# Searched network of a gated cross-attention stack: both halves of the probability transposes run back to back, each half in a score memory pair of its own

## The reference, cut to what matters

```python
for c in range(NUM_NOD):                     # 6 nodes
    q = ew[c, 0] * (nodes[in_q] @ We[eq] + be[eq])
    k = ew[c, 1] * (nodes[in_k] @ We[ek] + be[ek])
    v = ew[c, 2] * (nodes[in_v] @ We[ev] + be[ev])
    o = _mha(q, k, v, Wq[c], Wk[c], Wv[c], Wo[c])   # softmax(qh kh / sqrt(32)) vh, 8 heads, then @ wo
    nodes[c] = act_w[c] * o + q
...
return _layernorm(nodes[5], ln_g, ln_b)
```

## Time and profile before

| | |
|---|---|
| time, median of 3 runs | 3070.01 us |
| span of the profiled execution, first to last instruction | 3069.1 us |
| TensorE matmuls (PE) | 2945.7 us busy, 96% of the span |
| TensorE weight loads (PEld) | 2275.7 us, 74% |
| VectorE (DVE) | 2030.9 us, 66% |
| ScalarE (ACT) | 1448.5 us, 47% |
| GpSimd (POOL) | 650.4 us, 21% |
| searched network | about 816 to 1954 us of the span |

### The profile page before, as it was taken

How to read it: one execution, slowest core, us unless ns; L and a number is a source line. 1 busy time by engine, 2 the same in 40 slices (tenths; PEclk the granted TensorE clock), 3 DMA queues, 4 the chain that set the end, 5 groups by cost and what they waited for, 6 DMA issues and landing times. The chain is left out here.

```text
span 3069.1 us, 61161 instructions
## 1 busy us (share of the span) xinstructions
PE 2945.7 (96%) x23332; PEld 2275.7 (74%) x23332; DVE 2030.9 (66%) x4378; ACT 1448.5 (47%) x2845; POOL 650.4 (21%) x952
## 2 busy tenths in 40 slices
PE   8997999989899999999999999799999999899999
PEld 6874656567799999999999999577777777556444
DVE  5773111138577887788888877566767666589664
ACT  3431111126455555555555555476666666556000
POOL 4565000046100220013012200212212112036000
PEclk9997999999899999999999999899999999899999
DMA  9643233249300000000000000000000000337100
GB/s 292 214 128 106 82 117 110 88 144 299 104 1 2 1 2 1 2 1 1 2 1 2 1 2 1 24 25 22 17 22 22 17 22 17 106 108 227 51 14 21
DMA packets 79537, 185.47 MB, mean 60 GB/s; under 512 B 12981, under 2 KB 23202, under 8 KB 78916
## 3 DMA queue, kind: packets, MB, share of 16 engines
q1 hardware_dynamic: 62708, 141.50, 14.3%
q10 hardware_dynamic: 10208, 25.30, 2.8%
q0 software_dynamic: 6336, 14.76, 1.7%
HBM read 150.26 MB, written 27.79 MB: 58 GB/s over the span
## 5 line engine op out<-in xcount | busy, mean ns | idle before, releaser
L2792 DVE CUSTOM_DVE_ANT_0 probs<-ps,add 112x375 f32<-112x375 f32 x512 | 258.9, 544 | 82.7 <-PE ps L2945 76.0
L2871 ACT ACTIVATE probs<-probs,neg_top 112x375 f32<-112x375 f32 x512 | 278.5, 600 | 63.5 <-DVE neg_top L2792 60.1
L1734 DVE TENSOR_TENSOR hidden<-gated,ps 128x512 f32<-128x512 f32 x64 | 44.0, 687 | 294.7 <-PE ps L1777 294.7
L2972 PEld LDWEIGHTS ps<-ident,probs 112*125 112x125 f32 x1536 | 196.8, 188 | 44.4 <-issue 16.7
L2351 DVE TENSOR_REDUCE top<-ps 112x16 f32<-112x1792 f32 x96 | 194.2, 2023 | 46.1 <-PE ps L2590 45.9
L2972 PE MATMUL ps<-ident,probs 112*125 112x112 f32 x1536 | 219.7, 279 | 1.8 <-DVE probs_t L2799 1.8
L3416 PE MATMUL ps<-we,xn_t 128*128 128x512 f32 x448 | 201.9, 614 | 1.7 <-PEq L846 0.9
L2367 DVE TENSOR_TENSOR probs<-probs,inv_sum 112x1792 f32<-112x1792 f32 x96 | 196.0, 2042 | 3.3
L2355 DVE TENSOR_TENSOR probs<-ps,top 112x1792 f32<-112x1792 f32 x96 | 194.3, 2024 | 3.3
L2363 DVE TENSOR_REDUCE row_sum<-probs 112x16 f32<-112x1792 f32 x96 | 193.9, 2020 | 3.2 <-ACT probs L2475 3.2
L2558 PE MATMUL ps<-ident,probs 112*112 112x112 f32 x1536 | 179.8, 260 | 8.2 <-ACT probs_t L2470 7.3
(11 more groups left out here) (464 smaller groups left out, 6276.8 us busy)
## 6 DMA issues: line engine op xcount, KB each, us to landing
ctx_t<-in_ctx_T_dram SPq DMA_DIRECT2D x96, 375.0 KB, 4.5
ctx_sb<-in_ctx_dram ACTq DMA_DIRECT2D x64, 384.0 KB, 4.5
ctx_sb<-in_ctx_dram SPq DMA_DIRECT2D x32, 384.0 KB, 8.9
ctx_sb<-in_ctx_T_dram SPq DMA_DIRECT2D x32, 375.0 KB, 3.1
queue<-zeros SPq DMA_DIRECT2D x32, 256.0 KB, 5.1
rows<-queue SPq DMA_DIRECT2D x16, 512.0 KB, 4.9
outputs<-out SPq DMA_DIRECT2D x16, 512.0 KB, 2.9
mask_in<-in_mask_BxSxS_fk_dram SPq DMA_DIRECT2D x16, 328.1 KB
```

The source lines that it names most:

```text
L2792: dve.tensor_tensor_reduce(out=probs[:, u, h, :], in0=k.ps[0:S, SCORE + h, 0:L], in1=add[:, j % 2, :], scale=1.0, scalar=BIG, op0=ALU.add, ...
L2871: act.activation(probs[:, u, h, :], probs[:, u, h, :], ACT.Exp, bias=neg_top[:, u, h:h + 1], scale=-1.0).then_inc(s["probs_done"], 1)
L2972: mm = pe.transpose(k.ps[0:KR, PT + h % 2, r * S:(r + 1) * S], probs[:, n % 3, h, r * KR:(r + 1) * KR], k.ident[0:S, 0:S])
```

## The change

The second half of the transposes moves up, next to the first half, and gets banks 2 and 3 (two of the four score banks) in place of 6 and 7. For that it waits until VectorE has finished with the scores of item t-1 (`diff_done`), and `scores(t)` waits until ScalarE has copied both halves out. On ScalarE the second copy moves up next to the first too, ahead of `copy_node`.

```diff
--- before.py
+++ after.py
@@ -2222,7 +2222,7 @@
         inv_sum = sb(nc, "inv_sum", [S, 4, PAIR * HQ], F32)
         att_t = sb(nc, "att_t", [P, DC, PS], F32)
 
-        EVEN, ODD, SCORE, PT = 0, 1, 2, 6
+        EVEN, ODD, SCORE, PT = 0, 1, 2, (6, 2)
         ROUND_ITEMS = NODES * STREAMS
         GROUPS = ITERS * STREAMS
         ITEMS = ITERS * ROUND_ITEMS
@@ -2468,7 +2468,7 @@
                     if m:
                         act.wait_ge(s["att_done"], m)
                     act.activation(probs_t[:, b, :, :].rearrange("p (o i) t -> p o (i t)", o=2),
-                                   k.ps[0:S, PT:PT + 2, 0:HEADS // 2 * S], ACT.Copy).then_inc(s["probs_t_copied"], 1)
+                                   k.ps[0:S, PT[b]:PT[b] + 2, 0:HEADS // 2 * S], ACT.Copy).then_inc(s["probs_t_copied"], 1)
 
                 def exp(m):
                     act.wait_ge(s["diff_done"], m + 1)
@@ -2483,6 +2483,7 @@
                         exp(t - 1)
                     if 0 <= t - 2 < ITEMS:
                         copy_probs_t(t - 2, 0)
+                        copy_probs_t(t - 2, 1)
                     if t in input_at:
                         copy_input(input_at[t])
                     if t in final_at:
@@ -2490,7 +2491,6 @@
                     if 0 <= t - 3 < ITEMS:
                         copy_node(t - 3)
                     if 0 <= t - 2 < ITEMS:
-                        copy_probs_t(t - 2, 1)
                         copy_att(t - 2)
 
             @block.tensor
@@ -2552,10 +2552,14 @@
 
                 def transpose_probs(m, b):
                     pe.wait_ge(s["probs_normed"], m + 1)
-                    if m or b:
-                        pe.wait_ge(s["probs_t_copied"], PAIR * m + b)
+                    if b == 0 and m:
+                        pe.wait_ge(s["probs_t_copied"], PAIR * m - 1)
+                    if b == 1:
+                        pe.wait_ge(s["diff_done"], min(m + 2, ITEMS))
+                        if m:
+                            pe.wait_ge(s["probs_t_copied"], PAIR * m)
                     for h in range(HEADS):
-                        mm = pe.transpose(k.ps[0:S, PT + h // 4, h % 4 * S:(h % 4 + 1) * S],
+                        mm = pe.transpose(k.ps[0:S, PT[b] + h // 4, h % 4 * S:(h % 4 + 1) * S],
                                           probs[:, m % 2, h % 4, b * HQ + h // 4, :], k.ident[0:S, 0:S])
                     mm.then_inc(s["probs_transposed"], 1)
 
@@ -2582,6 +2586,8 @@
                         pe.wait_ge(s["input_copied"], STREAMS)
                     else:
                         pe.wait_ge(s["diff_done"], m)
+                    if m >= 2:
+                        pe.wait_ge(s["probs_t_copied"], PAIR * (m - 1))
                     for b in range(PAIR):
                         for q in range(HQ):
                             for r in range(4):
@@ -2613,6 +2619,7 @@
                         project(t)
                     if 0 <= t - 2 < ITEMS:
                         transpose_probs(t - 2, 0)
+                        transpose_probs(t - 2, 1)
                     if t in input_at:
                         odd_free(t)
                         transpose_input(input_at[t])
@@ -2623,8 +2630,6 @@
                         transpose_final(final_at[t])
                     if 0 <= t - 3 < ITEMS:
                         project_out(t - 3)
-                    if 0 <= t - 2 < ITEMS:
-                        transpose_probs(t - 2, 1)
                     if t < ITEMS:
                         scores(t)
                     if 0 <= t - 2 < ITEMS:
```

## The result

The changed kernel takes 3079.0 us (median of 20 runs, 3074.08 to 3090.32) against 3072.26 us for the kernel before (20 runs, 3067.80 to 3082.03). The ratio is 1.002 with a 95% interval of 1.0012 to 1.0027: 4 to 8 us slower. A second batch gave 1.0025 (1.0016 to 1.0035).

What follows compares the result with a forecast made beforehand. TensorE's own instruction train was taken to set the pace, 11.42 us a slot. Terms 0 + 15.8 - 4.3 - 0.8 + 0.4 = +11.1 us on 3070.0 gave 3081.1 us, range 3065 to 3098.

Steps and rivals of the forecast that it cites:

- TensorE's own work: Ordinary slots: no instruction added or removed, and the joints between trains sum to no difference, 0 us.
- Waits added: Ordinary slots: second eight wait for VectorE's subtraction, scores for the second copy; both covered by other work, 0 us.
- The wait that moves: Attend, slots 3 to 95: copy_node ends 0.77 us later and holds attend 0.17 us in 93 slots, +15.8 us.
- Rival (c): Attend in each slot: release after copy_node always takes 0.40 us; +27.9 us, 3097.9 us; chance 0.14.
- (a): Attend in ordinary slots: copy_node is just in time and attend isn't held; -4.7 us, 3065.3 us; chance 0.26.
- Extra transposes: In 24 slots the second eight cover four extra transposes' wait for VectorE's copy of the values, 0.18 each, -4.3 us.
- Filling: Third slot, pipeline filling: scores start 0.8 us earlier after the new waits, -0.8 us.
- Draining: Last slots, pipeline draining: in slot 97 copy_node ends later and attend ends at 1942.45 instead of 1942.00, +0.4 us.
- Rival (d): Ordinary slots: second eight become the bound, held by VectorE's subtraction; 3090 us for the first tenth; chance 0.03.
- Rival (b): Third slot and slot 96: waits for the first copy also vanish without a substitute; 3058.4 us; chance 0.04.

Runs made afterwards that it cites:

- att_bank6: The changed kernel with attend written to bank 6 instead of bank 0, no longer waiting for copy_node; 3067.2 us, ratio 0.9986 to the kernel before.
- before_again: The kernel before, run and profiled once more without any edit; ratio 1.0005 to the kernel before.
- before_padded_13: The kernel before plus seven unused VectorE reductions at the network's end, lengthening it by 13.0 us; 3077.47 us, ratio 1.0013 to the kernel before.
- order alone: The changed kernel with both transpose halves ahead of project_out but both in banks 6 and 7 as before; 3203.78 us, one run.

## Why the prediction was right, and where it was not

The time of 3079.0 us lies in the range and near the forecast of 3081, and the direction was the forecast's. The mechanism, attend held by copy_node, was right. That the number came so near is in part luck: the sum was 11.1 us on a base of 3070.0, while the kernel before took 3072.26 in the 20 runs beside the changed one, so the difference was 6.7 us (4 to 8 by the ratio), on the edge of the 0.2% from which the prediction called it slower; and errors of both signs cancelled, as the steps show:

- **TensorE's own work, 0.** Right: 1.53 for sixteen transposes and 3.14 up to the scores, as worked out from a slot without transposes. (The prediction's 94 slots of 11.42 us are 93, and 24 of them, those with extra transposes, take 12.04 to 12.07 us before; its sum counts 93.)
- **Waits added, 0.** Right for the ordinary slots: neither appears in the view of waits from 1000 to 1900 us.
- **The wait that moves, +15.8.** Right: 91 of the 93 slots lie between the fifth and the last project, and att_bank6 took 15.2 us off there, 0.167 each; 93 make 15.5. The release was taken as 0.22, halfway between 0.06 and 0.40, and it was 0.22 to 0.23 in nearly every slot. The size was luck: the row of 0.40 was one of a kind. In before_again the same place of the unchanged kernel reads

```profile
1944.78 0.79 ACT L2441 ACTIVATE last<-ps,bo 128x224 f32<-128x224 f32 x2 [2.06 <-PE ps L2575]
...
1945.79 0.38 PEld L2605 LDWEIGHTS ps<-probs_t,v 112*32 112x32 f32 x16 [0.50 <-issue]
```

That is 1945.57 to 1945.79, 0.22, and before_padded_13 has 0.23 there. A second profile of the kernel before would have given the price without guessing. The 50 to 100 ns that the Trainium skill gives for reading a semaphore (Advanced Engine Details and Errata, Network/Comms) did not cover what passes between the end of the copy and attend's load. The trace records two separate waiting instructions of 0.05 us each in that distance, so it does not speak against the figure for one read. Rival (c), 0.40 throughout, fell with (a).
- **Extra transposes, -4.3.** Mis-sized: 9.5 - 15.2 leaves -5.7, 0.24 for each of 24 slots instead of 0.18. I had counted the wait for `v` alone; the joint behind it closed too. From the four extra transposes to project_out it was 1702.96 - 1702.48 = 0.48 us before and is 0.44 after, and over both kinds of slot the distance shrinks by 0.05 to 0.06. Before, then after:

```profile
1702.96 0.92 PE L2573 MATMUL ps<-nodes,wq 128*128 128x224 f32 x4
```

```profile
1708.82 0.60 PE L2514 MATMUL ps<-ident,last 128*112 128x128 f32 x4
...
1709.26 0.92 PE L2577 MATMUL ps<-nodes,wq 128*128 128x224 f32 x4
```

- **Filling, -0.8.** Right for the third slot, and then lost: from first to fifth project the two kernels took 40.3 and 41.1 us before, 40.8 and 40.7 after. The third slot took 16.16 us before and 15.33 after, 0.83 less, in both profiles of each. The fourth gave it back: 11.53 and 11.79 us before, 12.35 and 12.32 after. It starts earlier, so more of its key projection falls into a stretch at the lower clock that ends at 848.7 us before and 848.4 after, by the clock records: the key projection takes 1.72 us before (the query projection starts at 850.17) and 2.38 after (849.17). Before, then after:

```profile
848.45 1.89 PE L2525 MATMUL ps<-nodes,wkh 128*128 128x224 f32 x8
```

```profile
846.79 2.54 PE L2525 MATMUL ps<-nodes,wkh 128*128 128x224 f32 x8
```

- **Draining, +0.4.** Mis-sized: +3.4. I moved the idle time of slot 96 without asking what the clock does after it; nearly all of the next 7.5 us ran at the lower level, and project_out then ended behind VectorE's normalisation.
- **What was missing, -6.4 behind the network.** No step of mine looked past the network. The shortfall from 11.1 to the measured 6.7 is this: 15.5 - 5.7 + 3.4 + 0 = 13.2, measured 13.0 between the means of two profiles each, less 6.4.

Rival (d), the second eight held by the subtraction, has nothing in the profile of the ordinary slots; only the third slot and slot 96 show it. Rival (b), the gap for the copy as the gain, did not come true. In the third slot the wait of 5.30 us became two, of 2.77 and 2.39, and in slot 96 one of 2.46 took the place of 1.97. That copy does cost TensorE 1.10 us of idling a slot when both halves share banks and stand side by side (order alone), but the old order hid it beneath project_out for nothing.

## What to carry to other kernels

Moving work to the front of a train does not only hide its own wait; the work that it overtakes ends later, and each buffer that this work or its reader frees comes free later. Here a copy that was done 0.85 us ahead of attend's start now ends 0.08 us ahead of where attend would start (1508.90 and 1508.98 in att_bank6), and the 0.2 us from one engine's end to another's start, invisible until then, became 0.17 us in each of 93 slots. Where a stage is filled to 99.9% by one engine, look for the next wait with less slack than what you moved is long, and see whether a bank that has just come free takes it away.

## What the runs showed of the hardware

- **The same work takes another time with the place at which the clock falls.** The same instructions behind the network take 144.3 or 137.9 us, at a mean granted clock of 0.91 or 0.95; 140.9 and 147.5 us were seen too. The two profiles of one kernel agree, for both kernels profiled twice. 13.0 us of useless work ahead turned 144.3 into 137.9. A change measured by the time of a long program thus carries a term that has nothing to do with it, here half its size; the network's own length (1138 to 1151 us) tells what the edit did.
- **A release costs more than a tenth of a microsecond.** From the end of ScalarE's copy to attend's first load it took 0.22 to 0.23 us, in nearly all of the 93 slots, where project_out starts 0.06 after its copy. The trace records two waiting instructions of 0.05 us each ahead of attend's load and none ahead of project_out's, which carries its wait itself. Whether that is the reason was not tried.
